# Attention stage of a two-branch network: 64-column streams for mixing, outputs and logits, a fourth buffer of rows, projection four blocks ahead

## The chip, the cores and the metric

One core of one Trainium2 chip runs the whole program in one launch. The metric is device time in microseconds, from start to end of the program. Before the change three runs gave a median of 3651.51 us (3636.55 to 3661.43).

## What is computed

The input is x, 8 images of 56 x 56 positions with 128 channels, float32. Two branches follow each other, each on a group-normalized x and each added to x. The first is a gated long convolution (projection, a two-dimensional FFT written as matrix products, taps made by a small network). The change does not touch it. The second is the attention, cut here to what matters:

```python
xs = _gn(x).reshape(b, n, c)                     # b = 8, n = 3136 tokens, c = 128
q, k, v = xs @ Wq.T, xs @ Wk.T, xs @ Wv.T; v = v + v
# each as (b, n, 8 heads, 16); all three divided by their norm over the 16
attn_head = softmax(einsum('bnhd,bngd->bnhg', v_h, v_h))      # 8 x 8 for each token
q = einsum('bnhg,bngd->bnhd', attn_head, q)                   # the same for k
attn = softmax(einsum('bnhd,bnhe->bnde', k, q))               # 16 x 16 for each token
out = einsum('bnhd,bnde->bnhe', v, attn)                      # then @ proj_w.T + proj_b
```

All the matrices of the attention are tiny: 8 x 8 over heads and 16 x 16 over features, one of each for every token.

## The kernel before, in words

`build` runs six stages one after the other. The last, `attend` (its constants at L993 to L1002), is the one that changes. It starts some 2.2 ms into the program and lasts till the end.

**Blocks and units.** The 25,088 tokens are cut into `NB` = 56 blocks of 448 tokens (4 groups of 112). A block is projected to q, k, v, normalized, and stored to HBM in a head-major form (`v_heads`, `qk_heads`). It is then loaded again in the layout the small products need: `v_blocks` holds, block-diagonally, the v rows of 16 tokens and their heads, and `qk_rows` holds the q, the constant 1, the k and the norm of v, 34 numbers for each (token, head) row. Half a block, 14 groups of 16 tokens, is a unit; there are `NU` = 112.

**Rounds.** Every engine runs the same hand-written loop over rounds i. TensorE does, in this order: `scores(i+1)` (L1117 to L1127), one projection `project(bk)` (L1104), `mix(i)` (L1129), `outputs(i-2)` (L1152), `project(bk+1)`, `logits(i-1)` (L1141) and, in 8 rounds of every 14, `final` (L1163: the output projection of an eighth of an image and the addition of x). A float32 matmul appears as two matmul instructions and two weight loads in the trace. Per unit:

- scores: 28 matmuls, 128 rows by 64 columns of weights, streaming 64 columns. Alternate matmuls use output partitions 0 to 63 and 64 to 127.
- mixing: 28 matmuls of 64 rows by 64 columns of weights, streaming `QKM` = 33 columns (16 of q, the 1, 16 of k). Alternate matmuls use both another half of the rows and another half of the output partitions. All write one PSUM bank.
- logits: 56 matmuls of 32 rows by 64 columns, streaming 16. The four that belong to a group use the four quarters of the rows. Two of them write bank 0 of `ps_l` (one in each half of the partitions), two write bank 1.
- outputs: 28 matmuls of 128 rows by 64 columns, streaming 16.

**The other engines.** ScalarE (`act`) does per round `root` (in even rounds; a square root, with a change of table on either side), `exp_s(i+1)`, `copy_in(bk)` (two squares and a copy of the projection out of its single PSUM bank, L1207 to L1209), `leave_mix(i)`, `copy_in(bk+1)`, `exp_l(i-1)`, and the store of a finished piece. The second projection of a round can't start before `copy_in(bk)` has emptied the bank (`qkv_read`). VectorE does `mask(i+1)`, `weigh(i)`, `leave(i-2)`, `divide(i-1)`, `squares`, in odd rounds `clamp`, in even rounds `normalize` (L1277 to L1288), which makes the rows that go to HBM, and `add_bias` (L1333). GpSimd masks `k_blocks` (L1100).

**The DMA order.** SyncE's queue does for every block n: `load_xn(n+3)` (L1060, the input of a later projection), once per image the load of `x1` (L1089), and `turn(n)`. `turn` waits until `normalize(n)` is done, issues the two stores (L1065, L1066), waits until the buffer `n % NIN` is free, which is when `leave` of the block `NIN` earlier has run (`o_r`), waits for the stores to land, and issues nine loads (L1077 eight times, L1078). `AHEAD` = 3 blocks are projected before the first scores, and the projection stays that far ahead; `NIN` = 3 buffers hold `v_blocks` and `qk_rows`.

Of the kernel before, what the change touches and what calls it, by code (L numbers as in the profile page):

```python
# [988 lines left out]
def attend(nc, t, k):  # L989

    TB, BPB, GB, GU = 112, 4, 28, 14
    NB = BATCH * TOK // (TB * BPB)
    NU = 2 * NB
    UPI = NU // BATCH
    AHEAD = 3
    NIN = 3
    RPI = TOK // 16  # L1000
    RH = RPI // 2
    with ExitStack() as ctx:  # L1002
# [15 lines left out]
        kb = [sb(f"k_blocks{m}", [128, GU, HD, 4]) for m in range(2)]  # L1018
        qk = [sb(f"qk_rows{m}", [128, GB, QKW]) for m in range(NIN)]
        ex = [sb(f"s_exp{m}", [128, GU, 64]) for m in range(2)]  # L1020
        eb = [sb(f"e_blocks{m}", [128, GU, 64]) for m in range(2)]
        dsq, wgt = ([sb(f"{n}{m}", [128, GU, 1]) for m in range(2)] for n in ("d_sq", "d_sq_inv"))
        qm = [sb(f"q_mixed{m}", [128, GU, HD]) for m in range(2)]
        km = [sb(f"k_mixed{m}", [128, GU, HD]) for m in range(2)]
        pe_ = [sb(f"p_exp{m}", [128, 2, GU, HD]) for m in range(2)]
        zs, zi = ([sb(f"{n}{m}", [128, 2, GU]) for m in range(2)] for n in ("z_sum", "z_inv"))
        pn = [sb(f"p_norm{m}", [128, 2, GU, HD]) for m in range(2)]
        oT = [sb(f"oT{m}", [128, HD, RPI]) for m in range(2)]
        x1 = [sb(f"x1_in{m}", [128, TOK]) for m in range(2)]
        res = [sb(f"res{m}", [RH, 4, CH]) for m in range(4)]  # L1030
# [4 lines left out]
        in_loaded = [sem(f"in_loaded{m}") for m in range(NIN)]  # L1035
        x1_loaded = [sem(f"x1_loaded{m}") for m in range(2)]
        out_stored = [sem(f"out_stored{m}") for m in range(4)]
# [16 lines left out]
        @block.sync  # L1054
        def _(sp):
            def load_xn(n):
                if n >= 3:
                    sp.wait_ge(qkv_ps, (n - 2) * BPB)
                b, c = n // NCH, n % NCH
                sp.dma_start(xn[n % 3][:], t.XN[b, :, c * BPB * TB:(c + 1) * BPB * TB]).then_inc(xn_loaded[n % 3], 16)  # L1060

            def turn(n):
                sp.wait_ge(st_r, n + 1)
                at = slice(n * BPB * TB, (n + 1) * BPB * TB)
                sp.dma_start(t.VT[at].rearrange("(j p) x -> p j x", p=TB), st_v[n % 2][:]).then_inc(st_stored[n % 2], 16)  # L1065
                sp.dma_start(t.QK[at].rearrange("(j p) h x -> p j (h x)", p=TB), st_qk[n % 2][:].rearrange("p j h x -> p j (h x)")).then_inc(st_stored[n % 2], 16)  # L1066
                m = n % NIN
                if n < NIN:
                    sp.wait_ge(cleared, m + 1)
                else:  # L1070
                    sp.wait_ge(o_r, 2 * (n - NIN) + 2)
                sp.wait_ge(st_stored[n % 2], 32 * (n // 2 + 1))
                v = t.VT[at].rearrange("(g r a q) (d h) -> a q d g r h", q=4, r=2, a=2, h=HEADS)
                for a in range(2):
                    for q in range(4):
                        at8 = (4 * a + q) * HEADS
                        sp.dma_start(vb[m][64 * a + q:64 * a + 64:4, :, :, at8:at8 + HEADS], v[a, q]).then_inc(in_loaded[m], 16)  # L1077
                sp.dma_start(qk[m][:], t.QK[at].rearrange("(g n) h x -> (n h) g x", n=16)).then_inc(in_loaded[m], 16)  # L1078

            for n in range(3):  # L1080
                load_xn(n)
            for n in range(NB):
                if n + 3 < NB:
                    load_xn(n + 3)
                if n % NCH == 3:
                    b = n // NCH
                    if b > 1:
                        sp.wait_ge(f_ps, 8 * (b - 1))
                    sp.dma_start(x1[b % 2][:], t.X1[b]).then_inc(x1_loaded[b % 2], 16)  # L1089
                turn(n)  # L1090

        @block.gpsimd
        def _(pool):
            for m in range(NIN):
                pool.memset(vb[m][:], 0.0).then_inc(cleared, 1)
            for i in range(NU):
# [6 lines left out]
        def _(pe):  # L1103
# [25 lines left out]
            def mix(i):  # L1129
# [5 lines left out]
                for g, gb in groups(i):  # L1135
                    for a in range(2):
                        rows = slice(64 * a, 64 * a + 64)
                        last = pe.matmul(ps_m[rows, g * QKM:(g + 1) * QKM], eb[i % 2][rows, g, :], qk[n % NIN][rows, gb, 0:QKM], start=True, stop=True)  # L1138
                last.then_inc(m_ps, 1)

            def logits(i):  # L1141
# [4 lines left out]
                for g in range(GU):  # L1146
                    for s in range(4):
                        rows, half = slice(32 * s, 32 * s + 32), 64 * (s % 2)
                        last = pe.matmul(ps_l[half:half + 64, s // 2, g * HD:(g + 1) * HD], kb[i % 2][rows, g].rearrange("p d m -> p (d m)"), qm[i % 2][rows, g, :],  # L1149
                                         start=True, stop=True)  # L1150
                last.then_inc(l_ps, 1)

            def outputs(i):
# [4 lines left out]
                for g, gb in groups(i):  # L1158
                    for a in range(2):
                        last = pe.matmul(ps_o[64 * a:64 * a + 64, g * HD:(g + 1) * HD], vb[n % NIN][:, gb, a, :], pn[i % 2][:, a, g, :], start=True, stop=True)  # L1160
                last.then_inc(o_ps, 1)

            def final(b, u):  # L1163
                lo, e0 = u // 4 * RH, u % 4 * 4
                if u == 0:
                    pe.wait_ge(o_r, (b + 1) * UPI)
                    pe.wait_ge(x1_loaded[b % 2], 16 * (b // 2 + 1))
                if b * 8 + u:
                    pe.wait_ge(f_r, b * 8 + u)
                for e in range(4):  # L1170
                    to = ps_f[0:RH, e * CH:(e + 1) * CH]
                    pe.matmul(to, oT[b % 2][:, e0 + e, lo:lo + RH], k.w[:, PW, :], start=True, stop=False)  # L1172
                    at = (e0 + e) * RPI + lo
                    last = pe.matmul(to, x1[b % 2][:, at:at + RH], k.ident[:], start=False, stop=True)  # L1174
                last.then_inc(f_ps, 1)
# [22 lines left out]
        def _(act):  # L1198
# [12 lines left out]
            def root(n):  # L1211
                act.wait_ge(nsc_r, n + 1)
                act.activation(nrm[n % 2][:], nsc[n % 2][:], ACT.Sqrt).then_inc(nrm_r, 1)

            def exp_s(i):
                act.wait_ge(s_ps, i + 1)
# [19 lines left out]
            def store(b, u):  # L1236
                act.wait_ge(f_r, b * 8 + u + 1)
                lo, e0 = u // 4 * RH, u % 4 * 4
                rows = t.out_rows[b * TOK:(b + 1) * TOK].rearrange("(e r) c -> r e c", e=HD)
                act.dma_start(rows[lo:lo + RH, e0:e0 + 4, :], res[u % 4][:]).then_inc(out_stored[u % 4], 16)  # L1240

            for bk in range(AHEAD * BPB):
                copy_in(bk)
                if bk % BPB == BPB - 1 and bk // BPB + 1 < AHEAD:
                    root(bk // BPB)
            exp_s(0)
            for i in range(ROUNDS + 1):
# [3 lines left out]
                if unit(i + 1):  # L1251
                    exp_s(i + 1)
                if bk < NB * BPB:
                    copy_in(bk)
# [12 lines left out]
        def _(dve):  # L1267
# [29 lines left out]
            def weigh(i):  # L1297
# [6 lines left out]
                if i >= 2:  # L1304
                    dve.wait_ge(l_ps, i - 1)
                dve.tensor_tensor(qm[a][:], ps[:, :, 0:HD], wgt[a][:].to_broadcast([128, GU, HD]), ALU.mult).then_inc(q_r, 1)

            def divide(i):
# [6 lines left out]
                if i >= 2:  # L1315
                    dve.wait_ge(o_ps, i - 1)
                dve.tensor_tensor(pn[a][:], pe_[a][:], bcast(zi[a][:], 3, HD), ALU.mult).then_inc(p_r, 1)  # L1317

# [15 lines left out]

            for m in range(2):
                dve.memset(st_qk[m][:, :, :, HD:HD + 1], 1.0)
            for pr in range(AHEAD * 2):
# [6 lines left out]
            for i in range(ROUNDS):  # L1344
# [15 lines left out]
                if i in FINS:  # L1360
                    add_bias(*FINS[i])


# [88 lines left out]
```

## Time and profile before

| | before |
|---|---|
| runs, median of 3 | 3651.51 us (3636.55 to 3661.43) |
| profiled execution, its own time | 3654.92 us |
| its span | 3653.1 us |
| mean granted clock of TensorE in it | 0.90 of full speed |
| TensorE matmul busy | 3309.5 us (91%) |
| TensorE weight loads busy | 2525.6 us (69%) |
| VectorE / ScalarE / GpSimd busy | 2089.4 / 1480.1 / 246.4 us |

The busy share of TensorE is the time in which at least one matmul was under way. Matmuls are pipelined, so it says nothing of how fast they follow each other; the distance between the starts of two groups does. A granted clock of 1.00 is 2.4 GHz, 0.50 is 1.2 GHz, and a value between is a mixture over the stretch. In a timeline each row is a group of equal instructions of one engine in order of time, with its start, its length, and in brackets the idle time before it and what ended it. SPq and ACTq are DMA issues of SyncE and of ScalarE. Times are us from the start of the span.

### The profile page before, as it was taken

The numbers are of one execution on the slowest core, as the hardware profiler recorded it, in microseconds if no ns is written. First come the engines' busy times: TensorE is split into PE (matmuls) and PEld (weight loads), VectorE is DVE, ScalarE is ACT, GpSimd is POOL, SyncE is SP. The second block draws the span as 40 slices with busy tenths as digits, with TensorE's granted clock in tenths as the row PEclk, the third lists the DMA queues.
The fourth block names the chain that finished last, engine by engine and source line by source line (L and its number), as shares of the span: only waits on it lengthen the run. The fifth ranks groups of instructions, "written<-read, shape, count | busy, mean of one in ns | idle before, by whom it ended". The sixth has DMA issues, their size and how long they took to land. (4 is left out here: it accounts for less than half of the span.)

```text
span 3653.1 us, 106250 instructions
## 1 busy us (share of the span) xinstructions
PE 3309.5 (91%) x44223; PEld 2525.6 (69%) x44223; DVE 2089.4 (57%) x3836; ACT 1480.1 (41%) x3256; POOL 246.4 (7%) x157
## 2 busy tenths in 40 slices
PE   5776978999999999999999895889898989999998
PEld 4553324777777777777777442778787878878787
DVE  4453453666666667666667573445555555455553
ACT  3554412444444444444443443434444444443440
POOL 0000000000000000000000122111111111111110
PEclk9787967999999999999999896879898989898887
DMA  6885004111111221111111993545555555554552
GB/s 149 242 231 144 1 0 156 48 48 49 49 48 48 50 50 49 47 49 49 48 48 45 385 391 108 93 67 105 80 107 92 90 98 89 90 90 93 87 90 42
DMA packets 1033977, 351.34 MB, mean 96 GB/s; under 512 B 888569, under 2 KB 1005991, under 8 KB 1028519
## 3 DMA queue, kind: packets, MB, share of 16 engines
q1 hardware_dynamic: 763952, 251.80, 29.6%
q10 hardware_dynamic: 269687, 94.47, 10.1%
q8 instruction: 281, 4.60, 0.5%
q14 instruction: 57, 0.47, 0.0%
HBM read 174.01 MB, written 172.15 MB: 95 GB/s over the span
## 5 line engine op out<-in xcount | busy, mean ns | idle before, releaser
L751 ACT ACTIVATE x_half<-ps_x 56x228 f32<-56x228 f32 x1024 | 365.1, 357 | 673.4 <-PE ps_x L693 664.3
L801 DVE TENSOR_TENSOR terms<-spec,ps_z 112x456 f32<-112x456 f32 x1024 | 572.8, 621 | 38.0 <-PE ps_z L701 33.1
L708 PEld LDWEIGHTS ps_q<-inv_w,prod 112*114 112x114 f32 x4096 | 434.9, 180 | 27.9 <-issue 25.5
L708 PE MATMUL ps_q<-inv_w,prod 112*114 112x112 f32 x4096 | 451.0, 263 | 1.4 <-DVE prod L805 1.4
L701 PE MATMUL ps_z<-x_half,fwd_w 120*112 120x456 f32 x1024 | 447.0, 559 | 0.8
L811 DVE COPY y_sb<-ps_y 112x224 f32<-112x224 f32 x256 | 100.0, 390 | 414.6 <-PE ps_y L716 331.6
L1126 PE MATMUL ps_s<-v_blocks 128*64 128x64 f32 x6272 | 264.5, 256 | 76.7 <-DMA qk_rows<-qk_heads 72.7
L1126 PEld LDWEIGHTS ps_s<-v_blocks 128*64 128x64 f32 x6272 | 246.5, 169 | 93.2 <-DMA qk_rows<-qk_heads 78.4
L1149 PEld LDWEIGHTS ps_l<-q_mixed,k_blocks 32*64 32x64 f32 x12544 | 232.4, 152 | 91.7 <-issue 75.2
L1100 POOL TENSOR_TENSOR k_blocks<-k_mixed,same_of 128x896 f32<-128x896 f32 x112 | 192.0, 1714 | 1175.2 <-ACT k_mixed L1234 1175.2
L1311 DVE TENSOR_REDUCE z_sum<-p_exp 128x28 f32<-128x448 f32 x112 | 69.4, 620 | 348.1 <-ACT p_exp L1225 348.1
L1149 PE MATMUL ps_l<-q_mixed,k_blocks 32*64 32x16 f32 x12544 | 246.5, 218 | 23.7 <-issue 23.3
L1110 PE MATMUL ps_qkv<-weights,xn_in 128*112 128x384 f32 x448 | 230.3, 600 | 38.8 <-ACT qkv L1209 25.3
L693 PEld LDWEIGHTS ps_x<-fwd_h,v_in 96*120 96x120 f32 x2048 | 257.7, 186 | 8.5 <-issue 3.7
L693 PE MATMUL ps_x<-fwd_h,v_in 96*120 96x114 f32 x2048 | 257.6, 269 | 1.7 <-ACT x_half L751 1.7
L716 PEld LDWEIGHTS ps_y<-q_half,inv_h 114*112 114x112 f32 x1024 | 179.0, 176 | 115.2 <-issue 94.5
L701 PEld LDWEIGHTS ps_z<-x_half,fwd_w 120*112 120x112 f32 x1024 | 160.9, 177 | 124.9 <-issue 111.9
L1138 PEld LDWEIGHTS ps_mix<-qk_rows,e_blocks 64*64 64x64 f32 x6272 | 197.7, 138 | 68.0 <-issue 67.3
L716 PE MATMUL ps_y<-q_half,inv_h 114*112 114x224 f32 x1024 | 236.6, 353 | 1.3 <-ACT q_half L778 1.3
L1295 DVE TENSOR_TENSOR e_blocks<-s_exp,same_of 128x896 f32<-128x896 f32 x112 | 122.0, 1089 | 174.2 <-ACT s_exp L1219 171.6
L1160 PE MATMUL ps_o<-p_norm,v_blocks 128*64 128x16 f32 x6272 | 211.9, 213 | 5.4 <-DVE p_norm L1317 4.7
L1219 ACT ACTIVATE s_exp<-ps_s 128x896 f32<-128x896 f32 x112 | 102.7, 917 | 272.4 <-PE ps_s L1126 271.9
(120 smaller groups left out, 4699.0 us busy)
## 6 DMA issues: line engine op xcount, KB each, us to landing
conv_in<-v_sb ACTq DMA_DIRECT2D x112, 256.0 KB, 3.3
v_in<-conv_in SPq DMA_DIRECT2D x256, 112.0 KB
qk_heads<-st_qk SPq DMA_DIRECT2D x56, 476.0 KB, 4.2
qk_rows<-qk_heads SPq DMA_DIRECT2D x56, 476.0 KB, 6.9
conv_out<-y_sb ACTq DMA_DIRECT2D x512, 49.0 KB
y<-conv_out SPq DMA_DIRECT2D x8, 1792.0 KB, 13.0
x_in<-in_x SPq DMA_DIRECT2D x8, 1568.0 KB, 9.6
shortcut<-short ACTq DMA_DIRECT2D x8, 1568.0 KB, 6.3
```

The source lines that it names most:

```text
L693: last = pe.matmul(ps_x[0:120, c * 2 * NF:(c + 1) * 2 * NF], v_in[b % 2][:, c * 2 * PADW:c * 2 * PADW + 120], k.fwd_h[:], start=True, stop ...
L701: last = pe.matmul(ps_z[b % 2][x][0:NFFT, 0:PC], k.fwd_w[:, x, :], x_half[b % 2][:].rearrange("p c a f -> p (c a f)"), start=True, stop=True)
L708: last = pe.matmul(ps_q[0:2 * NF, c * NFFT:(c + 1) * NFFT], prod[b % 2][:, x, c * 2 * NF:(c + 1) * 2 * NF], k.inv_w[:, x, :], start=(x == ...
L716: last = pe.matmul(ps_y[0:2 * SIDE, 0:CC // 2 * SIDE], k.inv_h[:, x, :], q_half[:, :, x, :], start=(x == 0), stop=(x == 1))
L751: last = act.activation(x_half[b % 2][to:to + SIDE, :, a], src, ACT.Copy)
L801: last = dve.tensor_tensor(terms[:, x, :], spec[a][:, s, :], ps_z[b % 2][z][0:NFFT, 0:PC], ALU.mult)
L1100: pool.tensor_tensor(kb[i % 2][:], bcast(km[i % 2][:], 3, 4), bcast(bcast(k.same4[:], 1, HD), 1, GU), ALU.mult).then_inc(k_r, 1)
L1110: pe.matmul(ps_a[0:TB, 0:3 * CH], xn[n % 3][:, j * TB:(j + 1) * TB], k.w[:, WQ:WQ + 3, :].rearrange("p a c -> p (a c)"), start=True, stop= ...
L1126: last = pe.matmul(to, v[:, gb, a, :], v[:, gb, a, :], start=True, stop=True)
L1138: last = pe.matmul(ps_m[rows, g * QKM:(g + 1) * QKM], eb[i % 2][rows, g, :], qk[n % NIN][rows, gb, 0:QKM], start=True, stop=True)
L1149: last = pe.matmul(ps_l[half:half + 64, s // 2, g * HD:(g + 1) * HD], kb[i % 2][rows, g].rearrange("p d m -> p (d m)"), qm[i % 2][rows, g, :],
L1160: last = pe.matmul(ps_o[64 * a:64 * a + 64, g * HD:(g + 1) * HD], vb[n % NIN][:, gb, a, :], pn[i % 2][:, a, g, :], start=True, stop=True)
```

## The change

1. `mix`, `logits` and `outputs` stream 64 columns instead of 33, 16 and 16. The extra columns read the rows of the next groups and write into the PSUM columns of the next groups, which the next matmuls overwrite. The tiles that are read get room behind their last group (`qk_rows` one group, `q_mixed` and `p_norm` three), cleared once at the start. Every matmul keeps its weights, rows and partitions.
2. `NIN` goes from 3 to 4, and `AHEAD` from 3 to 4.
3. The two stores of a block's heads move from SyncE's queue to ScalarE's: in the prologue behind the projections of the next block, in the loop in odd rounds behind `exp_s(i+1)` and ahead of `copy_in(bk)`. ScalarE waits there for `normalize` (`st_r`).
4. `x1` has one buffer instead of two. ScalarE loads it, at the start and behind the last store of each image; SyncE no longer does.

The diff, without the sizes of the tiles and the renamed semaphores:

```diff
-    AHEAD = 3
-    NIN = 3
+    AHEAD = 4
+    NIN = 4
...
-        x1 = [sb(f"x1_in{m}", [128, TOK]) for m in range(2)]
+        x1 = sb("x1_in", [128, TOK])
...
             def turn(n):
-                sp.wait_ge(st_r, n + 1)
                 at = slice(n * BPB * TB, (n + 1) * BPB * TB)
-                sp.dma_start(t.VT[at].rearrange("(j p) x -> p j x", p=TB), st_v[n % 2][:]).then_inc(st_stored[n % 2], 16)
-                sp.dma_start(t.QK[at].rearrange("(j p) h x -> p j (h x)", p=TB), st_qk[n % 2][:].rearrange("p j h x -> p j (h x)")).then_inc(st_stored[n % 2], 16)
...
             for n in range(NB):
                 if n + 3 < NB:
                     load_xn(n + 3)
-                if n % NCH == 3:
-                    b = n // NCH
-                    if b > 1:
-                        sp.wait_ge(f_ps, 8 * (b - 1))
-                    sp.dma_start(x1[b % 2][:], t.X1[b]).then_inc(x1_loaded[b % 2], 16)
                 turn(n)
...
             for m in range(NIN):
+                pool.memset(qk[m][:, GB:, :], 0.0)
                 pool.memset(vb[m][:], 0.0).then_inc(cleared, 1)
...
-                        last = pe.matmul(ps_m[rows, g * QKM:(g + 1) * QKM], eb[i % 2][rows, g, :], qk[n % NIN][rows, gb, 0:QKM], start=True, stop=True)
+                        last = pe.matmul(ps_m[rows, g * QKM:g * QKM + 64], eb[i % 2][rows, g, :], strided(qk[n % NIN][rows], gb * QKW, [[1, 64]]), start=True, stop=True)
...
-                        last = pe.matmul(ps_l[half:half + 64, s // 2, g * HD:(g + 1) * HD], kb[i % 2][rows, g].rearrange("p d m -> p (d m)"), qm[i % 2][rows, g, :],
+                        last = pe.matmul(ps_l[half:half + 64, s // 2, g * HD:g * HD + 64], kb[i % 2][rows, g].rearrange("p d m -> p (d m)"), qm[i % 2][rows, g:g + 4, :],
                                          start=True, stop=True)
...
-                        last = pe.matmul(ps_o[64 * a:64 * a + 64, g * HD:(g + 1) * HD], vb[n % NIN][:, gb, a, :], pn[i % 2][:, a, g, :], start=True, stop=True)
+                        last = pe.matmul(ps_o[64 * a:64 * a + 64, g * HD:g * HD + 64], vb[n % NIN][:, gb, a, :], pn[i % 2][:, a, g:g + 4, :], start=True, stop=True)
...
+            def store_heads(n):
+                at = slice(n * BPB * TB, (n + 1) * BPB * TB)
+                act.wait_ge(st_r, n + 1)
+                act.dma_start(t.VT[at].rearrange("(j p) x -> p j x", p=TB), st_v[n % 2][:]).then_inc(st_stored[n % 2], 16)
+                act.dma_start(t.QK[at].rearrange("(j p) h x -> p j (h x)", p=TB), st_qk[n % 2][:].rearrange("p j h x -> p j (h x)")).then_inc(st_stored[n % 2], 16)
+
...
                 act.dma_start(rows[lo:lo + RH, e0:e0 + 4, :], res[u % 4][:]).then_inc(out_stored[u % 4], 16)
-
+                if u == 7 and b + 1 < BATCH:
+                    act.dma_start(x1[:], t.X1[b + 1]).then_inc(x1_loaded, 16)
+
+            act.dma_start(x1[:], t.X1[0]).then_inc(x1_loaded, 16)
             for bk in range(AHEAD * BPB):
                 copy_in(bk)
-                if bk % BPB == BPB - 1 and bk // BPB + 1 < AHEAD:
-                    root(bk // BPB)
+                if bk % BPB == BPB - 1:
+                    if bk // BPB + 1 < AHEAD:
+                        root(bk // BPB)
+                    if bk // BPB:
+                        store_heads(bk // BPB - 1)
             exp_s(0)
             for i in range(ROUNDS + 1):
...
                 if unit(i + 1):
                     exp_s(i + 1)
+                if i % 2 == 1 and i // 2 + AHEAD - 1 < NB:
+                    store_heads(i // 2 + AHEAD - 1)
                 if bk < NB * BPB:
                     copy_in(bk)
```

## Rows read from the trace of the kernel before

**Rows 1.** Windows: us, busy of each engine, clock, DMA share, GB/s
```profile
2275.60:3592.50 1316.90, 1210.47 (x31954) 1039.33 (x31954) 687.86 (x1248) 555.38 (x1237) 188.66 (x110) 0.86 0.52 90
...
2782.50:2786.00 3.50, 3.50 (x138) 2.91 (x139) 2.04 (x4) 1.98 (x8) 1.68 (x1) 1.00 0.63 71
2787.50:2790.00 2.50, 0.94 (x18) 0.95 (x20) 2.43 (x5) 0.00 (x0) 0.00 (x0) 0.50 0.53 112
```

**Rows 2.** Timeline of TensorE, one round without final, at full clock
```profile
2742.69 1.85 PE L1126 MATMUL ps_s<-v_blocks 128*64 128x64 f32 x56
2744.47 0.90 PE L1110 MATMUL ps_qkv<-weights,xn_in 128*112 128x384 f32 x2
2745.30 1.82 PE L1138 MATMUL ps_mix<-qk_rows,e_blocks 64*64 64x33 f32 x56
2747.05 1.81 PE L1160 MATMUL ps_o<-p_norm,v_blocks 128*64 128x16 f32 x56
2748.79 0.90 PE L1110 MATMUL ps_qkv<-weights,xn_in 128*112 128x384 f32 x2
2749.62 1.82 PE L1149 MATMUL ps_l<-q_mixed,k_blocks 32*64 32x16 f32 x112
2751.37 0.45 PE L1126 MATMUL ps_s<-v_blocks 128*64 128x64 f32 x7
```

**Rows 3.** Timeline of TensorE, a final at full clock, up to the next scores
```profile
2683.01 0.46 PE L1172 MATMUL ps_fin<-weights,oT 128*98 128x128 f32 x2
2683.30 0.38 PE L1174 MATMUL ps_fin<-ident,x_in 128*98 128x128 f32 x2
2683.52 0.38 PE L1172 MATMUL ps_fin<-weights,oT 128*98 128x128 f32 x2
...
2684.93 1.85 PE L1126 MATMUL ps_s<-v_blocks 128*64 128x64 f32 x56
```

**Rows 4.** Groups by line, TensorE matmuls, 2275.6 to 3592.5 (three of seven)
```profile
L1126 PE MATMUL ps_s<-v_blocks 128*64 128x64 f32 x6218 | 261.6, 256 | 76.7 <-DMA qk_rows<-qk_heads 72.7 <-issue 3.0 <-ACT s_exp L1219 1.0
L1149 PE MATMUL ps_l<-q_mixed,k_blocks 32*64 32x16 f32 x12208 | 238.1, 217 | 23.7 <-issue 23.3
L1110 PE MATMUL ps_qkv<-weights,xn_in 128*112 128x384 f32 x424 | 211.0, 582 | 11.3 <-ACT qkv L1209 11.2
```

**Rows 5.** Timeline of TensorE around a fall of the clock at 2786.6
```profile
2784.76 1.82 PE L1149 MATMUL ps_l<-q_mixed,k_blocks 32*64 32x16 f32 x112
2789.06 3.26 PE L1126 MATMUL ps_s<-v_blocks 128*64 128x64 f32 x56 [2.48 <-DMA qk_rows<-qk_heads]
2792.24 1.48 PE L1110 MATMUL ps_qkv<-weights,xn_in 128*112 128x384 f32 x2
```

**Rows 6.** Timeline, an even round that follows a round without final
```profile
2587.45 1.85 PE L1126 MATMUL ps_s<-v_blocks 128*64 128x64 f32 x56
...
2594.39 0.90 PE L1110 MATMUL ps_qkv<-weights,xn_in 128*112 128x384 f32 x2 [0.68 <-ACT qkv L1209]
```

**Rows 7.** Timeline, the odd round behind it: from the exponential to the stores
```profile
2598.28 0.54 ACT L1225 ACTIVATE p_exp<-ps_l 128x448 f32<-128x448 f32 x1 [1.98 <-PE ps_l L1149]
...
2603.26 0.68 DVE L1288 TENSOR_TENSOR st_v<-qkv,rnorm 112x512 f32<-112x512 f32 x1
...
2604.33 0.49 SPq L1066 DMA_DIRECT2D qk_heads<-st_qk  x1
```

**Rows 8.** Timeline of SyncE's queue, the loads of the same block
```profile
2610.53 7.71 SPq L1077 DMA_DIRECT2D v_blocks<-v_heads  x8
2618.28 1.35 SPq L1078 DMA_DIRECT2D qk_rows<-qk_heads  x1
```

**Rows 9.** The page's part 6: DMA issues, KB each, us to landing
```profile
qk_rows<-qk_heads SPq DMA_DIRECT2D x56, 476.0 KB, 6.9
```

**Rows 10.** Timeline of TensorE, the last projection ahead and the first scores
```profile
2263.75 1.62 PE L1110 MATMUL ps_qkv<-weights,xn_in 128*112 128x384 f32 x2 [1.07 <-ACT qkv L1209]
2275.62 0.69 PE L1126 MATMUL ps_s<-v_blocks 128*64 128x64 f32 x7 [10.26 <-DMA qk_rows<-qk_heads]
```

More of the change, by code:

```diff
@@ L1018, in attend @@
         kb = [sb(f"k_blocks{m}", [128, GU, HD, 4]) for m in range(2)]
-        qk = [sb(f"qk_rows{m}", [128, GB, QKW]) for m in range(NIN)]
+        qk = [sb(f"qk_rows{m}", [128, GB + 1, QKW]) for m in range(NIN)]
         ex = [sb(f"s_exp{m}", [128, GU, 64]) for m in range(2)]
@@ L1022, in attend @@
         dsq, wgt = ([sb(f"{n}{m}", [128, GU, 1]) for m in range(2)] for n in ("d_sq", "d_sq_inv"))
-        qm = [sb(f"q_mixed{m}", [128, GU, HD]) for m in range(2)]
+        qm = [sb(f"q_mixed{m}", [128, GU + 3, HD]) for m in range(2)]
         km = [sb(f"k_mixed{m}", [128, GU, HD]) for m in range(2)]
@@ L1026, in attend @@
         zs, zi = ([sb(f"{n}{m}", [128, 2, GU]) for m in range(2)] for n in ("z_sum", "z_inv"))
-        pn = [sb(f"p_norm{m}", [128, 2, GU, HD]) for m in range(2)]
+        pn = [sb(f"p_norm{m}", [128, 2, GU + 3, HD]) for m in range(2)]
         oT = [sb(f"oT{m}", [128, HD, RPI]) for m in range(2)]
-        x1 = [sb(f"x1_in{m}", [128, TOK]) for m in range(2)]
+        x1 = sb("x1_in", [128, TOK])
         res = [sb(f"res{m}", [RH, 4, CH]) for m in range(4)]
@@ L1035, in attend @@
         in_loaded = [sem(f"in_loaded{m}") for m in range(NIN)]
-        x1_loaded = [sem(f"x1_loaded{m}") for m in range(2)]
+        x1_loaded = sem("x1_loaded")
         out_stored = [sem(f"out_stored{m}") for m in range(4)]
@@ L1077, in turn @@
                         sp.dma_start(vb[m][64 * a + q:64 * a + 64:4, :, :, at8:at8 + HEADS], v[a, q]).then_inc(in_loaded[m], 16)
-                sp.dma_start(qk[m][:], t.QK[at].rearrange("(g n) h x -> (n h) g x", n=16)).then_inc(in_loaded[m], 16)
+                sp.dma_start(qk[m][:, 0:GB, :], t.QK[at].rearrange("(g n) h x -> (n h) g x", n=16)).then_inc(in_loaded[m], 16)
             for n in range(3):
@@ L1166, in final @@
                     pe.wait_ge(o_r, (b + 1) * UPI)
-                    pe.wait_ge(x1_loaded[b % 2], 16 * (b // 2 + 1))
+                    pe.wait_ge(x1_loaded, 16 * (b + 1))
                 if b * 8 + u:
@@ L1173, in final @@
                     at = (e0 + e) * RPI + lo
-                    last = pe.matmul(to, x1[b % 2][:, at:at + RH], k.ident[:], start=False, stop=True)
+                    last = pe.matmul(to, x1[:, at:at + RH], k.ident[:], start=False, stop=True)
                 last.then_inc(f_ps, 1)
@@ L1305, in weigh @@
                     dve.wait_ge(l_ps, i - 1)
-                dve.tensor_tensor(qm[a][:], ps[:, :, 0:HD], wgt[a][:].to_broadcast([128, GU, HD]), ALU.mult).then_inc(q_r, 1)
+                dve.tensor_tensor(qm[a][:, 0:GU, :], ps[:, :, 0:HD], wgt[a][:].to_broadcast([128, GU, HD]), ALU.mult).then_inc(q_r, 1)
             def divide(i):
@@ L1316, in divide @@
                     dve.wait_ge(o_ps, i - 1)
-                dve.tensor_tensor(pn[a][:], pe_[a][:], bcast(zi[a][:], 3, HD), ALU.mult).then_inc(p_r, 1)
+                dve.tensor_tensor(pn[a][:, :, 0:GU, :], pe_[a][:], bcast(zi[a][:], 3, HD), ALU.mult).then_inc(p_r, 1)
             def leave(i):
@@ L1335, in _ @@
             for m in range(2):
+                dve.memset(qm[m][:, GU:, :], 0.0)
+                dve.memset(pn[m][:, :, GU:, :], 0.0)
                 dve.memset(st_qk[m][:, :, :, HD:HD + 1], 1.0)
```

## The prediction, made before the changed kernel was run

> **What bounds the kernel now.** I read the 40 slices first: TensorE is busy nearly throughout and its clock is below full only in the attention. A window over the loop of rounds, from the first scores to the last [rows 1], gives 1316.9 us, TensorE busy for 1210.5 of them, VectorE for 688, ScalarE for 555, mean clock 0.86. So TensorE is the bound, but the view doesn't say what its busy time is made of. The timeline of one undisturbed round does [rows 2]. The groups start at 2742.69, 2744.47, 2745.30, 2747.05, 2748.79, 2749.62, and the next round at 2751.37: 8.68 us with no gap. A final adds 1.92 us (2683.01 to 2684.93 [rows 3]). The window holds 110 rounds, 56 of them with a final. If all were like these it would last 110 x 8.68 + 56 x 1.92 = 1062 us. It lasts 255 us longer, and that is what can be won or lost here.
>
> The groups by line split the 255 [rows 4]. The window's idle time is 1316.9 - 1210.5 = 106 us. Waits for the loaded rows are 72.7 us, of which 10.3 lie before the first scores and outside the window [rows 10], so 62. Waits for ScalarE's copy of the projection are 11 us, plus 1 for an exponential. What is left, some 31 us, is marked issue, most of it inside the logits (23.3). The other 255 - 106 = 149 us are matmuls that take longer than in the undisturbed round. Rows 5 show how: at half clock the scores take 3.18 us (2789.06 to 2792.24), at full clock 1.78 [rows 2]. A mean clock of 0.86 means 28% of the window, 369 us, at 1.2 GHz; busy time there is half lost, which bounds the loss at 184 us, and idle time that fell into it brings it down to about the 149.
>
> **Why the clock falls.** The window from 2782.5 to 2786.0 has TensorE busy for all of its 3.50 us at 2.4 GHz; from 2787.5 the clock is 1.2 GHz [rows 1]. What ran before the fall was mixing, outputs, one projection and logits (2784.76 to about 2786.6 [rows 5]), then idle. The clock fell at the end of the logits, with no idle time ahead of the fall worth naming. In the other falls that I opened it is nearly always this sequence of groups that stream 33, 16 and 16 columns, and the clock comes back while scores (64 columns) and projections (384) run. The time of a group doesn't depend on how much it streams: 56 instructions take 1.78 us with 64 columns, 1.75 with 33, 1.74 with 16, and 112 take 1.75 in the logits [rows 2]. The weight loads of 64 columns set the pace, and the array's streaming side lies idle in three groups of four while the engine counts as busy. I take that as the cause of the falls.
>
> **The Trainium skill says otherwise on one point.** "TensorE: Matmul & The Clock Gate", section "Why this matters for your kernels", asks for one thing to avoid drops in the middle of a kernel: no idle gap between bursts of matmuls. By that rule wide streams change nothing, and only the shorter waits of part 2 would help. Rows 1 don't bear it out, as the fall came at the end of a full window. It is rival B.
>
> **The change, part by part.**
>
> 1. *64 columns.* If weight loads go on setting the pace, each of the three groups comes to the pace of the scores, 1.78 us: +0.03, +0.04 and +0.03, 0.1 us a round, 12 us over 112 rounds. For mixing and logits this needs the streams of different row groups to run side by side. Rows 3 price one stream: two matmuls of 128 columns in 0.22 us (2683.30 to 2683.52), 0.86 ns a column, 55 ns for 64. The scores make two such streams in 1.78 / 28 = 64 ns, so two halves of the output do run side by side. No row shows it for streams in different rows; of weight loads it is shown, since the logits load four row groups in 1.75 / 28 = 62 ns. Bounds: +12 us if all run side by side, +300 if two that share a bank take turns (rival A); below zero nothing, as the weight loads stay. I take 12, being nearest to the scores' row. The gain is the clock: of the 149 us I keep 15 for falls that come with real idle time. Bounds: 0 to 149 left.
>
> 2. *Fourth buffer, projection four blocks ahead.* Today the heads of a block are done at 2603.94 [rows 7], the loads are issued from 2610.53 to 2619.63 [rows 8] and the last lands 6.9 us later [rows 9], 22 to 23 us after the heads. They are needed three rounds after the even round in which the heads are made, which at 9 to 10.6 us a round leaves about 20 us. So the wait comes again and again. With `AHEAD` = 4 they are needed five rounds after, and the buffer is free in time: about 40 us for 22. SyncE's queue needs 9.1 us for these loads, of about 21 us in two rounds, so it isn't the bound even if the projection's input took it as long. I take 10 of the 62 us as left; bounds 0 and 62. The first scores wait 10.26 us for rows now [rows 10]. Four more projections at 2.69 us (1.62 and the 1.07 ahead of it) take 10.8 us, which that wait covers; with ScalarE's wait for the first heads and x1's load beside the first inputs I add 6 us. At the end two rounds lose their projections, and the last groups may run at full clock: -4.
>
> 3. *Stores on ScalarE.* This adds a wait. Behind it in ScalarE's order stands `copy_in(bk)`, for it the second projection waits, and behind that the logits. Take time from the moment the round could start. In an even round the second projection starts 2594.39 - 2587.45 = 6.94 us in [rows 6], against 6.10 undisturbed [rows 2]: the chain exponential, division, squares, root, exponential, copy costs 0.84 us already now, in rounds not preceded by a final. In an odd round the exponential starts at 2598.28 and the heads are ready at 2603.94 [rows 7]. It starts about 0.15 us after the logits' end, so the heads come 5.8 us in. Two issues on ScalarE take 0.33 + 0.49 us by SyncE's rows, 0.9 with the gap. The copies then hold the bank for 1.04 us. The second projection starts 7.8 us in, 1.7 late. A preceding final (1.92 us) covers both delays. Without one there are 27 even and 27 odd rounds: 27 x (0.84 + 1.7) = 69 us, against 12 now. Bounds 12 (if the heads come earlier than in that row) and 92 (1.7 in each of the 54 rounds). VectorE and GpSimd have a round to spare in both.
>
> 4. *x1.* One load an image, issued behind the last store of the image and needed seven rounds later: nothing. The issue stalls stay at 31 us.
>
> **Sum.** 1062 + 12 (width) + 15 (clock) + 10 (rows) + 31 (issue) + 69 (ScalarE) = 1199 us for 1317: -118. Ends: +6 - 4. Together -116 against the profiled execution's 3654.9 us: 3539, rounded to 3540. That execution is 3 us above the median of the runs, within their spread of 25, so I make no correction.
>
> **Rivals.**
>
> A. *Row groups that share a PSUM bank take turns in streaming: slower.* In mixing a pair then takes 2 x 55 = 110 ns instead of 63, and the group 28 x 110 = 3.08 us, +1.3. In the logits the two matmuls of each bank take turns and the banks run side by side: the same +1.3. A round is 2.65 us longer, 297 us in all; ScalarE's delay is hidden under it (-57). 3540 + 297 - 57 = 3780. It decides as soon as a stream is longer than half a pair's weight loads, some 31 ns or 36 columns; at 33 and 16 columns, before, it can't be seen, which is why the trace neither supports nor excludes it. Against it stands that weight loads of four row groups overlap. The Trainium skill, "TensorEngine Tiling", section "Restrictions and Gotchas", says that different row tiles can't access one PSUM bank at the same time, which is this rival's mechanism; no row here tests it. Chance 0.12.
>
> B. *The clock doesn't follow the columns*, so the change doesn't do what its first part is for. The 149 us stay, but slow rounds hide ScalarE's delay (about -40): 3540 + 134 - 40 = 3634. For it: some falls come with idle time. Against: 64-column groups bring the clock back. Chance 0.10.
>
> C. *The waits for rows stay* because the DMA engines, not the order, are late. Their share is 0.52 now [rows 1] and would be 0.52 x 1317 / 1199 = 0.57. 3540 + 52 = 3592. Chance 0.10.
>
> **How the numbers follow.** My own case has 0.68 and runs from 3458 (no clock loss, no waits for rows, ScalarE's delay as now: -15 - 10 - 57) to 3620 (half of the clock loss left, +60, and 30 us of waits, +20). The range 3465 to 3640 cuts that low end a little, takes in B and C, and leaves out A. What this kernel's measurement can tell from no change is about 1%, 37 us. Faster: 0.66 + 0.09 from C + 0.03 from B = 0.78. Same: 0.02 + 0.06 + 0.01 = 0.09. Slower: A and a rest of B, 0.13.
>
> **What the profile after would show.** Right: mean clock in the loop above 0.95; groups of 56 and 112 at 1.78 us or a little more from start to start; waits of the scores for `qk_rows` nearly gone; waits of the second projection for ScalarE near 70 us, in odd rounds most, and behind ScalarE's copy a wait for `st_v`. Wrong: mixing or logits near 3 us at full clock (A); the clock at 0.86 with falls behind 64-column groups (B); waits for `qk_rows` above 40 us (C).

## The result, and the profile after

The changed kernel took 3548.18 us (median of 4 runs, 3536.75 to 3558.14), the kernel before 3649.46 us beside it (3636.55 to 3661.43). The ratio is 0.9722, 95% interval 0.9676 to 0.9768: 2.8% faster, some 101 us. The forecast was 3540 us. The profiled execution took 3544.20 us, with a span of 3542.4.

Windows of the changed kernel over its loop, from the first scores to the last, and two short ones around a fall of the clock (columns as in [rows 1]):

```profile
2273.90:3489.80 1215.90, 1100.69 (x31945) 931.23 (x31944) 681.82 (x1247) 548.54 (x1226) 185.45 (x110) 0.98 0.55 94
...
2579.00:2582.40 3.40, 0.54 (x35) 0.41 (x27) 0.00 (x0) 0.00 (x0) 0.00 (x0) 1.00 0.59 202
2582.50:2585.00 2.50, 1.85 (x35) 1.73 (x36) 0.53 (x1) 1.09 (x2) 0.00 (x0) 0.50 0.40 24
```

The loop is 101.0 us shorter (1316.9 before [rows 1]), the part behind it 8.0 us (52.6 against 60.6), and the first scores come 1.7 us earlier. That is all of the 110.7 us between the two spans. The mean clock in the loop is 0.98 instead of 0.86.

TensorE's matmuls in the same stretch, by line (before: [rows 4]):

```profile
L1120 PE MATMUL ps_s<-v_blocks 128*64 128x64 f32 x6216 | 220.8, 228 | 35.0 <-issue 30.0 <-ACT s_exp L1219 4.9
L1143 PE MATMUL ps_l<-q_mixed,k_blocks 32*64 32x64 f32 x12208 | 216.5, 221 | 33.1 <-issue 33.0
L1132 PE MATMUL ps_mix<-qk_rows,e_blocks 64*64 64x64 f32 x6160 | 205.4, 220 | 6.4 <-issue 6.2
L1154 PE MATMUL ps_o<-p_norm,v_blocks 128*64 128x64 f32 x6048 | 202.7, 224 | 4.5 <-issue 4.3
L1104 PE MATMUL ps_qkv<-weights,xn_in 128*112 128x384 f32 x417 | 190.3, 538 | 34.0 <-ACT qkv L1203 33.5
L1166 PE MATMUL ps_fin<-weights,oT 128*98 128x128 f32 x448 | 90.0, 283 | 0.6 <-issue 0.6
L1168 PE MATMUL ps_fin<-ident,x_in 128*98 128x128 f32 x448 | 85.9, 273 | 1.7 <-issue 1.7
```

The wait for `qk_rows` is gone from the list: 72.7 us before, none after. The wait for ScalarE's copy went from 11 to 33.5 us. The idle time marked issue is time in which TensorE waited for nothing that the profile shows. The forecast held it at 31 us; here it adds up to 30.0 + 33.0 + 6.2 + 4.3 + 0.6 + 1.7 = 75.8 us.

A round of the changed kernel with nothing in its way but the copy (timeline of TensorE, to be laid beside [rows 2]):

```profile
3020.80 1.85 PE L1120 MATMUL ps_s<-v_blocks 128*64 128x64 f32 x56
3022.58 0.90 PE L1104 MATMUL ps_qkv<-weights,xn_in 128*112 128x384 f32 x2
3023.41 1.85 PE L1132 MATMUL ps_mix<-qk_rows,e_blocks 64*64 64x64 f32 x56
3025.19 1.85 PE L1154 MATMUL ps_o<-p_norm,v_blocks 128*64 128x64 f32 x56
3027.86 0.90 PE L1104 MATMUL ps_qkv<-weights,xn_in 128*112 128x384 f32 x2 [0.82 <-ACT qkv L1203]
3028.69 1.86 PE L1143 MATMUL ps_l<-q_mixed,k_blocks 32*64 32x64 f32 x112
3030.48 1.85 PE L1120 MATMUL ps_s<-v_blocks 128*64 128x64 f32 x56
```

Mixing takes 1.78 us from start to start (3023.41 to 3025.19), the logits 1.79 (3028.69 to 3030.48). The same groups took 1.75 and 1.75 with 33 and 16 columns. If streams of 55 ns took turns, each would take 3.08 us. So the streams of different row groups run side by side, also where they share a PSUM bank. Without waits a round is 1.78 + 0.83 + 1.78 + 1.78 + 0.83 + 1.79 = 8.79 us, 0.11 more than before. So an undisturbed loop would now last 110 x 8.79 + 56 x 1.92 = 1074 us.

The loops of the kernels below are split in the same way. The excess is the window's length over the undisturbed loop (1062 us with all three groups narrow, 1074 with all three wide). Rows, copy and issue are idle times of TensorE inside the loop by what ended them; the small waits for an exponential (1 to 6 us) are left out. The rest is the excess without all idle time: matmuls at half clock, and the part of each stall that the modelled ends of matmuls cover. The falls, and the time at 1.2 GHz in us, are taken from the trace's record of the granted clock. Half of that time is the most that the clock can have cost. Each row is one execution, the profiled one. It lies within 6 us of its kernel's median, but for e4, whose profiled execution (3534.1 us) is its slowest of four and 15 us above its median.

| kernel | loop | excess | rows | copy | issue | rest | falls | at 1.2 GHz | DMA share |
|---|---|---|---|---|---|---|---|---|---|
| before | 1317 | 255 | 62 | 11 | 31 | 149 | 49 | 371 | 0.52 |
| changed | 1216 | 142 | 0 | 34 | 76 | 26 | 5 | 39 | 0.55 |
| e1, width alone | 1267 | 193 | 97 | 11 | 32 | 51 | 21 | 102 | 0.54 |
| e2, order alone | 1294 | 232 | 0 | 15 | 46 | 165 | 46 | 376 | 0.52 |
| e4, stores on SyncE | 1199 | 125 | 4 | 8 | 80 | 32 | 10 | 41 | 0.56 |
| e5, without v loads | 1164 | 90 | 0 | 47 | 28 | 8 | 2 | 12 | 0.40 |
| e9, e4 with paced loads | 1176 | 102 | 4 | 8 | 63 | 25 | 7 | 31 | 0.57 |

### The profile page after: what moved, and what is told of

It is laid out like the page before. It is cut to its first block and busy times, and to the rows that moved or that the text cites. A ratio compares the mean times of both kernels' runs of the same rounds, so it can differ in the third digit from the quotient of the medians.

```text
span 3542.4 us, 106257 instructions
## 1 busy us (share of the span) xinstructions
PE 3186.1 (90%) x44223; PEld 2402.5 (68%) x44223; DVE 2085.8 (59%) x3840; ACT 1476.2 (42%) x3254; POOL 246.6 (7%) x162
## 5 line engine op out<-in xcount | busy, mean ns | idle before, releaser
L1104 PE MATMUL ps_qkv<-weights,xn_in 128*112 128x384 f32 x448 | 215.3, 564 | 72.6 <-ACT qkv L1203 56.0
L1143 PEld LDWEIGHTS ps_l<-q_mixed,k_blocks 32*64 32x64 f32 x12544 | 202.6, 135 | 99.6 <-issue 64.2
L1143 PE MATMUL ps_l<-q_mixed,k_blocks 32*64 32x64 f32 x12544 | 222.7, 221 | 35.9 <-issue 35.8
L1120 PE MATMUL ps_s<-v_blocks 128*64 128x64 f32 x6272 | 222.6, 228 | 35.0 <-issue 30.0
L1120 PEld LDWEIGHTS ps_s<-v_blocks 128*64 128x64 f32 x6272 | 203.0, 142 | 52.2 <-issue 35.2
L1154 PE MATMUL ps_o<-p_norm,v_blocks 128*64 128x64 f32 x6272 | 210.1, 224 | 9.6 <-DVE p_norm L1325 5.2
L1132 PE MATMUL ps_mix<-qk_rows,e_blocks 64*64 64x64 f32 x6272 | 209.3, 220 | 6.4 <-issue 6.2
L1201 ACT ACTIVATE sq<-ps_qkv 112x256 f32<-112x256 f32 x224 | 85.7, 383 | 304.4 <-PE ps_qkv L1104 162.3
```

Of the source, the lines that this page charges most:

```text
L1104: pe.matmul(ps_a[0:TB, 0:3 * CH], xn[n % 3][:, j * TB:(j + 1) * TB], k.w[:, WQ:WQ + 3, :].rearrange("p a c -> p (a c)"), start=True, stop= ...
L1120: last = pe.matmul(to, v[:, gb, a, :], v[:, gb, a, :], start=True, stop=True)
L1132: last = pe.matmul(ps_m[rows, g * QKM:g * QKM + 64], eb[i % 2][rows, g, :], strided(qk[n % NIN][rows], gb * QKW, [[1, 64]]), start=True, s ...
L1143: last = pe.matmul(ps_l[half:half + 64, s // 2, g * HD:g * HD + 64], kb[i % 2][rows, g].rearrange("p d m -> p (d m)"), qm[i % 2][rows, g:g ...
L1154: last = pe.matmul(ps_o[64 * a:64 * a + 64, g * HD:g * HD + 64], vb[n % NIN][:, gb, a, :], pn[i % 2][:, a, g:g + 4, :], start=True, stop=True)
```

## The experiments

### e1: the width alone

The kernel before with the three wide streams and the room behind the tiles that they read, and nothing else:

```diff
-  ps_m[rows, g * QKM:(g + 1) * QKM] ... qk[n % NIN][rows, gb, 0:QKM]
+  ps_m[rows, g * QKM:g * QKM + 64] ... strided(qk[n % NIN][rows], gb * QKW, [[1, 64]])
-  ps_l[..., g * HD:(g + 1) * HD] ... qm[i % 2][rows, g, :]
+  ps_l[..., g * HD:g * HD + 64] ... qm[i % 2][rows, g:g + 4, :]
-  ps_o[..., g * HD:(g + 1) * HD] ... pn[i % 2][:, a, g, :]
+  ps_o[..., g * HD:g * HD + 64] ... pn[i % 2][:, a, g:g + 4, :]
```

> The kernel before with the 64-column streams alone; three buffers, three blocks ahead, stores on SyncE. Theory (the clock follows the streamed columns): mean clock in the loop 0.96 or more, the clock loss of 149 us falls to 20 or less, while the waits for the rows stay at 62 us or grow to about 100, since rounds get shorter and the rows no sooner: 3560 to 3590 us. Rival B (the clock follows idle gaps only): clock near 0.87, time 3640 to 3665.

3587.23 us, ratio 0.9851 (0.9828 to 0.9874). Window over the loop and the scores' row:

```profile
2264.10:3531.00 1266.90, 1125.24 (x31952) 948.61 (x31952) 685.45 (x1248) 554.79 (x1237) 192.52 (x110) 0.96 0.54 94
```

```profile
L1127 PE MATMUL ps_s<-v_blocks 128*64 128x64 f32 x6216 | 233.7, 239 | 114.5 <-DMA qk_rows<-qk_heads 107.5 <-issue 5.6 <-ACT s_exp L1220 1.0
```

The clock came back, from 0.86 to 0.96, with three buffers and the old order. The waits for rows grew from 72.7 to 107.5 us (10.3 of either lie ahead of the loop). So the clock follows the columns, and part of what it gives goes into waiting for rows that come no sooner. The time is inside the theory's range. The loss to slow matmuls fell less than it said, to 51 us and not to 20. The 21 falls left are those of real idle time: each has 1.6 us of idle or more in the 3.5 us ahead of it. In the kernel before, 21 of the 49 falls have less than 0.5 us of idle in such a stretch.

### e2: the order alone

The changed kernel with the three lines of e1 turned back to 33, 16 and 16 columns.

> The changed kernel with the streams narrow again (33, 16 and 16 columns); fourth buffer, four blocks ahead and the stores on ScalarE stay. Theory: waits for rows gone, clock still 0.87 to 0.89 with falls that have no idle time before them, 3600 to 3630 us. Rival B (the gain is that of the shorter waits, and fewer gaps keep the clock up): clock above 0.95, 3545 to 3560 us.

3626.31 us, ratio 0.9953 (0.9919 to 0.9987). Window over the loop:

```profile
2274.70:3568.90 1294.20, 1226.76 (x31947) 1054.11 (x31946) 685.42 (x1247) 550.34 (x1226) 185.49 (x110) 0.85 0.52 89
```

The waits for rows are gone and the clock stays at 0.85, with 46 falls. The loss to slow matmuls even grew, from 149 to 165 us. Rival B is out: fewer gaps don't hold the clock while the streams are narrow. The time came out where the theory put it, at the upper end of its range, and the clock a little below its 0.87.

Alone the two parts give 0.5% and 1.5%, together 2.8%. The table shows why they are worth more together. In e2 the 62 us of waits for rows go, and 39 us come back: 15 of issue, 16 of slow matmuls, 9 of waits for ScalarE. In e1 the faster clock wins 98 us, and 35 us more are spent waiting for rows. The 0.5% is not that of lead and buffer alone, since e2 also holds the move of the stores, which costs time (e4). No run has lead and buffer alone with narrow streams.

### e6 and e7: which of the groups hold the clock

e6 is the changed kernel with only the logits back at 16 columns, e7 with mixing and outputs back at 33 and 16 and the logits wide.

> The changed kernel with the logits alone back at 16 columns; mixing and outputs stay at 64. Theory (what counts is the streaming of all that ran before): two of the three groups are enough to hold the clock most of the time: 5 to 20 falls in the loop instead of 5, mean clock 0.94 to 0.97, 3550 to 3575. Rival (the logits are what lets the clock fall, since the falls came at their end): 30 falls or more, clock under 0.91, 3590 or more.

3572.2 us, ratio 0.9796 (0.9748 to 0.9844), 31 falls, clock 0.94 in the loop. The time is inside the theory's range; the number of falls is the rival's.

> The changed kernel with the logits alone at 64 columns; mixing back at 33, outputs at 16. Theory: one wide group between two narrow ones holds the clock in part: 10 to 30 falls, mean clock 0.91 to 0.96, 3560 to 3600. Rival (the logits decide alone): 10 falls or fewer, clock above 0.96, within 12 us of the changed kernel.

3605.62 us, ratio 0.9874 (0.9824 to 0.9924), 46 falls, clock 0.91. More was lost than the theory gave. The windows over the two loops:

```profile
2271.40:3506.20 1234.80, 1138.22 (x31945) 969.69 (x31944) 683.70 (x1247) 549.48 (x1226) 185.38 (x110) 0.94 0.54 93
```

```profile
2271.00:3542.90 1271.90, 1164.15 (x31947) 986.38 (x31946) 681.33 (x1247) 548.37 (x1226) 185.38 (x110) 0.91 0.53 90
```

Counted by narrow groups, the loop's clock is 0.98 with none, 0.94 with one (logits), 0.91 with two, 0.85 with three (e2). Neither the logits nor the other two decide alone; each narrow group costs some of the clock.

### e5: is the fetch of instructions late behind the loads?

The idle time marked issue sits in the middle of groups of the same instruction, where nothing is waited for. An example from the changed kernel, just ahead of the fall in the windows above (timeline of TensorE):

```profile
2577.82 1.72 PE L1143 MATMUL ps_l<-q_mixed,k_blocks 32*64 32x64 f32 x99
2583.15 0.69 PE L1143 MATMUL ps_l<-q_mixed,k_blocks 32*64 32x64 f32 x13 [3.61 <-issue]
2583.78 3.25 PE L1120 MATMUL ps_s<-v_blocks 128*64 128x64 f32 x56
```

99 matmuls of the logits, 3.61 us of nothing, then the other 13, and scores at half clock. The profile has a DMA queue of kind instruction that moves 4.60 MB in 281 packets, 16 KB each. These packets tie the stalls to the fetch of TensorE's instructions. The loop has one for every 255 instructions of TensorE. In the changed kernel 67 stalls of more than 0.2 us lie inside a group. One is a wait for an exponential; the other 66 all end 1.2 to 1.8 us after the end of such a packet, a stretch that makes up 16% of the loop. In e5 the eight `v_blocks` loads of each block after the fourth are left out, so those blocks compute on old rows, and the scores wait for `qk_rows` alone:

```diff
-                for a in range(2):
+                for a in range(2 if n < NIN else 0):
```

> The changed kernel without the eight v_blocks loads of every block after the fourth (those blocks compute on the rows of the first four; qk_rows is still loaded). The changed kernel's idle time marked issue is 76 us against 31 before, in the middle of groups. Theory (TensorE's next instructions come late because their fetch, 16 KB by DMA, stands in line with the loads): DMA share falls from 0.55 to under 0.3, issue idle to 25 us or less, the time by 40 to 60 us, to about 3495. Rival (the fetch is late by itself, since TensorE at 2.4 GHz uses up a piece faster than the next is fetched): issue idle stays above 60 us, time within 15 us of the changed kernel.

3500.14 us, ratio 0.9599 (0.9552 to 0.9646). Window over the loop, the two rows that had most of the issue time, and that of the projections:

```profile
2278.70:3442.60 1163.90, 1082.27 (x31945) 917.87 (x31944) 680.64 (x1247) 548.22 (x1226) 185.39 (x110) 0.99 0.40 88
```

```profile
L1120 PE MATMUL ps_s<-v_blocks 128*64 128x64 f32 x6216 | 212.9, 225 | 17.3 <-issue 11.7 <-ACT s_exp L1219 5.5
L1143 PE MATMUL ps_l<-q_mixed,k_blocks 32*64 32x64 f32 x12208 | 209.8, 220 | 10.5 <-issue 10.5
L1104 PE MATMUL ps_qkv<-weights,xn_in 128*112 128x384 f32 x417 | 188.6, 534 | 47.7 <-ACT qkv L1203 47.4
```

Issue idle fell from 76 to 28 us, and the time by about 45. The DMA share fell less than expected, to 0.40. So most of the stalls come from the loads beside the fetch. The packets of instructions themselves take no longer beside the loads (0.97 us in the median, 1.06 in e5), so it is probably their start that comes late; what holds it is not shown. The wait for the copy rose from 33.5 to 47.4 us, probably because the stalls had covered a part of it.

### e3 and e4: the stores on ScalarE

e3 moves them behind the copy and `leave_mix` in the odd rounds; e4 gives them back to SyncE, ahead of the loads, and keeps four buffers and four blocks ahead.

```diff
# e3
-                if i % 2 == 1 and i // 2 + AHEAD - 1 < NB:
-                    store_heads(i // 2 + AHEAD - 1)
                 if bk < NB * BPB:
                     copy_in(bk)
                 if unit(i):
                     leave_mix(i)
+                if i % 2 == 1 and i // 2 + AHEAD - 1 < NB:
+                    store_heads(i // 2 + AHEAD - 1)
# e4
             def turn(n):
                 at = slice(n * BPB * TB, (n + 1) * BPB * TB)
+                sp.wait_ge(st_r, n + 1)
+                sp.dma_start(t.VT[at]..., st_v[n % 2][:]).then_inc(st_stored[n % 2], 16)
+                sp.dma_start(t.QK[at]..., st_qk[n % 2][:]...).then_inc(st_stored[n % 2], 16)
```

> The changed kernel with the two stores of a block on ScalarE moved behind copy_in and leave_mix of the odd rounds, so that the copy no longer waits for the heads. Theory (the stores' wait on ScalarE costs what the sum says): TensorE's wait for the copy falls from 56 us to 20 or less, the time by 25 to 35 us, to 3510 to 3525. Rival (what is won there is lost again to late instructions and other waits): within 8 us of the changed kernel.

3530.78 us, ratio 0.9699 (0.9665 to 0.9732), 8 us better than the changed kernel by the ratios and within their intervals. The wait for the copy did fall, to 9.8 us in the loop from 33.5 (the 56 us of the expectation counted the prologue's too):

```profile
L1104 PE MATMUL ps_qkv<-weights,xn_in 128*112 128x384 f32 x417 | 191.1, 540 | 9.8 <-ACT qkv L1203 9.8
```

In this loop the issue idle is 82 us. The theory had the mechanism and overrated its worth: in time the rival, within 8 us of the changed kernel, is the nearer one.

> The changed kernel with the two stores back on SyncE's queue, ahead of the loads, as before the change; four buffers and four blocks ahead stay. Theory: the fourth buffer and the lead alone take away the waits for rows, so they stay under 15 us, and TensorE's wait for the copy falls to 20 us: 3510 to 3530. Rival (the move of the stores is what brings the rows in time): waits for rows above 40 us and a time above 3560.

3519.34 us, ratio 0.9648 (0.9619 to 0.9676). The waits for rows are 4.0 us and the copy's 8.4:

```profile
L1123 PE MATMUL ps_s<-v_blocks 128*64 128x64 f32 x6218 | 221.3, 229 | 38.4 <-issue 33.4 <-DMA qk_rows<-qk_heads 4.0 <-ACT s_exp L1216 1.0
L1107 PE MATMUL ps_qkv<-weights,xn_in 128*112 128x384 f32 x417 | 191.4, 541 | 8.4 <-ACT qkv L1206 8.4
```

So the rows come in time without the move of the stores, and the move itself costs about 0.7%, near 27 us (0.9722 against 0.9648; the intervals just touch).

### e10 and e12: the lead and the buffer

Both are e4 with one constant turned back.

```diff
# e10
-    AHEAD = 4
+    AHEAD = 3
# e12
-    NIN = 4
+    NIN = 3
```

> The kernel of e4 with the projection three blocks ahead again and four buffers kept. Theory (both are needed, the heads come too late for three rounds whatever buffer is free): waits for rows come back to 50 to 110 us, time 3560 to 3600. Rival (the buffer was what was late): waits for rows under 20 us, time within 10 us of e4.

3647.29 us, ratio 1.0014 (0.9986 to 1.0043). Its scores' row:

```profile
L1123 PE MATMUL ps_s<-v_blocks 128*64 128x64 f32 x6218 | 238.5, 241 | 155.5 <-DMA qk_rows<-qk_heads 146.4 <-issue 8.0 <-ACT s_exp L1216 1.0
```

> The kernel of e4 with three buffers again and the projection four blocks ahead. With three blocks ahead and four buffers (e10) the waits for rows were 146 us. Theory (buffer and lead are both needed: with three buffers a block's loads start only when the unit two rounds before its first scores has left, some 20 us for loads of 16): waits for rows 30 to 80 us, 3545 to 3585. Rival (the lead alone does it): waits under 15 us, within 10 us of e4.

3583.39 us, ratio 0.9871 (0.9834 to 0.9909):

```profile
L1123 PE MATMUL ps_s<-v_blocks 128*64 128x64 f32 x6218 | 231.8, 237 | 94.6 <-DMA qk_rows<-qk_heads 85.6 <-issue 7.8 <-ACT s_exp L1216 1.0
```

Either constant alone brings the waits back. In e10 waits and time are far beyond the ranges that were written down; in e12 the waits are 6 us beyond theirs and the time is inside. Without the lead all of the gain is gone, though the clock is at 0.94 in this loop. What stays open is why e10, with four buffers, waits longer for rows than e1 does with three (136 us in the loop against 97). The two also differ in the `x1` buffer and its queue, and no run takes these apart.

### e8, e9 and e11: fewer late instructions?

e8 is e4 with the logits cut in halves and the second projection between them. e9 is e4 with the last four `v_blocks` loads and `qk_rows` held back by about a round. e11 is both.

```diff
# e8
+                if unit(i - 1):
+                    logits(i - 1, 0, GU // 2)
                 if bk < NB * BPB:
                     project(bk + 1)
                 if unit(i - 1):
-                    logits(i - 1)
+                    logits(i - 1, GU // 2, GU)
# e9
                 for a in range(2):
+                    if a and n >= NIN:
+                        sp.wait_ge(o_r, 2 * (n - NIN) + 3)
```

> The kernel of e4 (stores on SyncE) with the logits cut in two halves and the second projection of the round between them, so that TensorE uses up its instructions more evenly: four slow instructions stand between two runs of 112. Theory (a piece of instructions is late because a run of quick ones uses up the piece before): issue idle falls from 78 us in e4 to 45 to 60, the time by 15 to 30 us against e4. Rival (it is late for how long the fetch stands in line, whatever runs): issue idle stays at 70 us or more, time within 10 us of e4.

3520.2 us, ratio 0.9649 (0.9603 to 0.9695): no different from e4. The time is the rival's. Issue idle was 64 us instead of 80, a smaller fall than the theory wanted, and it can't be credited to the split. The profiled executions are e8's fastest (3503.8 us) and e4's slowest (3534.1), 30 us apart where the medians agree, so the 16 us may be the spread between executions of one kernel.

> The kernel of e4 with SyncE's loads of a block paced: the last four v_blocks loads and qk_rows wait until one more unit has left TensorE, about a round. The bytes stay the same. Theory (the fetch of instructions is late behind a burst of loads): with the burst cut in two the issue idle falls from 80 us in e4 to 55 or less, no new wait for rows above 15 us, the time by 15 to 30 us against e4. Rival (it is late by how many packets there are in all, not by how they are bunched): issue idle stays within 12 us of 80, time within 10 us of e4 or longer by waits for rows.

3505.68 us, ratio 0.9603 (0.9567 to 0.9640), the fastest kernel of this study that leaves nothing out. Issue idle is 63 us instead of 80 at the same DMA share (0.57 against 0.56), where the theory had 55 or less, and the waits for rows didn't grow:

```profile
L1125 PE MATMUL ps_s<-v_blocks 128*64 128x64 f32 x6216 | 217.4, 227 | 27.2 <-issue 21.9 <-DMA qk_rows<-qk_heads 3.9 <-ACT s_exp L1218 1.0
L1148 PE MATMUL ps_l<-q_mixed,k_blocks 32*64 32x64 f32 x12208 | 216.5, 221 | 27.7 <-issue 27.2
```

By the ratios this is 16 us against e4, with intervals that overlap. It is clearly better than the changed kernel and than the one before. Against e4 the 80 us come from that same slowest execution. That bunching matters is possible and not shown.

> The kernel of e9 with the logits split around the second projection, as in e8. In e8 the issue idle was 64 us against 80 in e4 with no time gained. Theory: the two effects add, issue idle 45 us or less, and the time 10 us or more under e4. Rival: as e9, within 8 us.

3516.29 us, ratio 0.9629 (0.9593 to 0.9666). Issue idle is 68 us and the time the rival's; no run shows a gain from the two together.

## Why the prediction was right

**The clock.** It was the largest term: 149 us, of which 15 were to be left. The loop's clock is 0.98 and 5 of 49 falls are left. The 39 us at 1.2 GHz in the table can have cost at most 19, so the 15 were about right; the rest of 26 us holds hidden parts of stalls too. e1 shows it as an effect of the width alone and e2 as absent without it. The rule of the Trainium skill ("TensorE: Matmul & The Clock Gate", "Why this matters for your kernels") is to leave no idle gap. It holds for what is left: the fall shown above lies within 3.61 us without a matmul, and each of the five has 1.9 us or more of idle in the 3.5 us ahead of it. It didn't cover the kernel before, where 21 of 49 falls came with less than 0.5 us of idle ahead of them, and e2, where gaps were few and the clock stayed low.

**The width.** +12 us in the sum, and 110 x 0.11 = 12 in the rows. Rival A would have made mixing and logits 3.08 us long; they take 1.78 and 1.79. The rule of the Trainium skill beside it ("TensorEngine Tiling", "Restrictions and Gotchas"), that different row tiles can't access one PSUM bank at the same time, doesn't hold for these groups. In mixing, two row groups write the same bank in different halves of the partitions, and they do so side by side.

**The rows.** 62 us, of which 10 were to be left; none are. The two reasons given, lead and free buffer, were both needed (e10, e12). The prologue's cost of 6 us wasn't there: the four projections more filled the first wait, and the first scores came 1.7 us earlier. What the sum had at -4 for the end was -8.

**ScalarE's wait, mis-sized.** The sum had 69 us. The mechanism and the single delay are as it put them. In this odd round the heads are finished at about 3069.4, the stores are issued, and the second projection starts 7.83 us after the round's start (3063.61 to 3071.44), where the sum said 7.8:

```profile
3063.61 1.85 PE L1120 MATMUL ps_s<-v_blocks 128*64 128x64 f32 x56
...
3068.73 0.69 DVE L1296 TENSOR_TENSOR st_v<-qkv,rnorm 112x512 f32<-112x512 f32 x1
...
3069.79 0.52 ACTq L1213 DMA_DIRECT2D qk_heads<-st_qk  x1
3070.41 0.38 ACT L1201 ACTIVATE sq<-ps_qkv 112x256 f32<-112x256 f32 x1 [3.99 <-DVE st_v L1296]
...
3071.44 0.90 PE L1104 MATMUL ps_qkv<-weights,xn_in 128*112 128x384 f32 x2 [1.59 <-ACT qkv L1203]
```

The number of rounds that pay it in full was too high. The sum had 27 odd rounds at 1.7 us; in the loop 40 rounds wait for the copy, 11 of them longer than 1.3 us, 33.5 us in all. Where instructions come late ahead of the second projection, that stall can cover the delay; with fewer such stalls, in e5, the wait is 47.4. That isn't all of it: e7 has 46.4 us with 56 us of issue idle.

**The issue idle, the step that failed.** "The issue stalls stay at 31 us." They are 76. I took them as a fixed toll. They are late fetches of instructions, and they depend on what the DMA engines do meanwhile: 28 us without the loads of `v_blocks` (e5). That they also depend on how fast TensorE uses up its instructions is read from the table and no run isolates it: 31 us before, 32 with the faster clock alone (e1), 46 with the shorter waits alone (e2), 76 with both.

In the sum's terms the errors nearly cancel: +45 (issue), -31 (ScalarE: 38 us, with the waits for an exponential, for 69), +11 (the rest of 26 for the clock's 15), -10 (rows), and about -12 at the two ends. The forecast of 3540 owes some of its closeness to that.

## What to carry to other kernels

A busy share of 90% or more doesn't mean a high clock: look at how much the busy matmuls stream, and where weight loads set the pace, stream up to their length, since here it cost 0.03 us a group and gave back 2.4 GHz. Price a faster clock together with the waits that follow next (here rows, then instructions), because each part alone gave 1.5% and 0.5% and both gave 2.8%. Before moving a DMA issue to an engine with other work, ask what stands behind its wait: here the rows came in time without the move.

## What the runs showed that was not expected

- The fetch of TensorE's own instructions shares the DMA engines with the data: idle time in the middle of groups was 31, 76 and 28 us in three kernels with the same number of TensorE instructions in the loop, the last of them without the loads of `v_blocks`. With the loads spread (e9) it was 63 us against 80 in e4, and whether that is the spreading is not shown.
- An issue of the `qk_heads` store takes ScalarE 0.51 us in the median and up to 1.73. 17 of the 56 take more than 0.9 us, and in 16 of these SyncE issues nothing at the time, so that is not the reason; it stays open. On SyncE, in the kernel before, 6 of 56 took more than 0.9 us. The median alone would hide this.
